# Two adjacency layers on one core: 66 tiles of the last stretch as three products of high and low halves

## What is computed

```
h  = relu(layernorm(x));   h1 = h @ W0 + B
S  = exp(-(1/adj - 1/mu)^2 / (2 sigma^2)) where adj < 0.5 off the diagonal, else 0
x1 = x + S @ h1
h  = relu(layernorm(x1));  h2 = h @ W1^T
out = x1 + (adj * adj + I) @ h2
```

## Time and profile before

| | us |
|---|---|
| median of 3 runs | 1929.82 (1929.51 to 1930.9) |
| the profiled execution | 1930.87 |
| its span | 1929.1 |
| TensorE busy (PE) | 1875.5 (97%) |
| weight loads (PEld, beside PE) | 845.5 (44%) |
| VectorE busy (DVE) | 1657.0 (86%) |
| ScalarE busy (ACT) | 1680.9 (87%) |
| DMA, over the span | 493.9 MB, 256 GB/s |

### The profile page before, as it was taken

The page is one execution under the profiler, slowest core; times in us unless marked ns, Lnnn a source line. Parts: engine busy times, 40 slices in busy tenths (PEclk is TensorE's granted clock), DMA queues, the critical chain, the costliest instruction groups (busy, mean ns, idle before and its releaser), DMA issues.

```text
span 1929.1 us, 12935 instructions
## 1 busy us (share of the span) xinstructions
PE 1875.5 (97%) x4576; PEld 845.5 (44%) x4576; DVE 1657.0 (86%) x937; ACT 1680.9 (87%) x967; POOL 87.3 (5%) x165
## 2 busy tenths in 40 slices
PE   7987989999999999999999999999999999999998
PEld 4543434444444444444444444444444444444443
DVE  7999999999999999999999999999999656556444
ACT  7999999999999999999999999999999755555421
POOL 0000000000000000000000000000000000000011
PEclk9999999999999999999999999999999999999999
DMA  7566677867877777766567766756555667877796
GB/s 265 197 223 234 246 290 258 296 249 287 291 291 272 292 267 266 260 236 251 218 250 267 258 248 216 262 194 234 195 195 197 241 262 270 317 276 297 265 371 237
DMA packets 78960, 493.90 MB, mean 256 GB/s; under 512 B 10160, under 2 KB 10544, under 8 KB 24880
## 3 DMA queue, kind: packets, MB, share of 16 engines
q1 hardware_dynamic: 66096, 451.11, 63.8%
q0 software_dynamic: 12800, 41.95, 5.7%
HBM read 469.96 MB, written 23.07 MB: 256 GB/s over the span
## 4 chain that ended last, share of the span: by engine, by line
ACT 63%; PE 27%; issue 5%; DVE 3%; DMA 1%; POOLq 0%; POOL 0%; SPq 0%; DVEq 0%
ACT rings L669 20%; ACT rings L674 19%; ACT rings L679 18%; PE p_x L415 14%; PE p_own L415 5%; PE p_l1b L397 4%; ACT rings L686 3%; PE p_l1a L397 2%; DVE rings L541 1%; DVE rings L548 1%; PE p_l1a L415 1%; DVE rings L559 1%; DMA x_buf<-xT 1%; ACT rstd_buf L715 0%; ACT rstd_buf L713 0%
## 5 line engine op out<-in xcount | busy, mean ns | idle before, releaser
L548 DVE SCALAR_TENSOR_TENSOR rings<-rings,small 128x2048 f32<-128x2048 f32 x256 | 600.0, 2344 | 56.1 <-ACT rings L674 55.1
L679 ACT ACTIVATE rings<-rings,small 128x2048 f32<-128x2048 f32 x256 | 532.6, 2080 | 63.5 <-DVE rings L548 63.5
L541 DVE SCALAR_TENSOR_TENSOR rings<-rings 128x2048 f32<-128x2048 f32 x256 | 584.4, 2283 | 0.6
L415 PE MATMUL p_x<-rings,h 128*128 128x512 f32 x1208 | 539.3, 596 | 10.2 <-DVE xa_buf L622 5.2
L669 ACT ACTIVATE rings<-rings,small 128x2048 f32<-128x2048 f32 x256 | 509.2, 1989 | 8.0 <-DVE rings L541 6.9
L559 DVE TENSOR_TENSOR rings<-rings 128x2048 f32<-128x2048 f32 x170 | 388.1, 2284 | 127.2 <-PE p_x L415 72.0
L674 ACT ACTIVATE rings<-rings 128x2048 f32<-128x2048 f32 x256 | 487.7, 1905 | 4.9
L397 PE MATMUL p_l1b<-rings,h 128*128 128x512 f32 x1024 | 464.3, 598 | 14.9 <-ACT rings L679 14.7
L397 PE MATMUL p_l1a<-rings,h 128*128 128x512 f32 x1024 | 461.0, 595 | 5.0 <-ACT rings L679 3.9
L415 PEld LDWEIGHTS p_x<-rings,h 128*128 128x128 f32 x1208 | 230.7, 191 | 302.8 <-issue 290.9
L415 PE MATMUL p_own<-rings,h 128*128 128x512 f32 x784 | 351.9, 592 | 0.0
(11 more groups left out here) (73 smaller groups left out, 327.5 us busy)
## 6 DMA issues: line engine op xcount, KB each, us to landing
rings<-adjT SPq DMA_DIRECT2D x422, 1024.0 KB, 5.3
xa_buf<-acc_dram POOLq DMA_DIRECT2D x61, 256.0 KB, 5.7
acc_dram<-xa_buf POOLq DMA_DIRECT2D x56, 256.0 KB, 5.5
x_buf<-xT SPq DMA_DIRECT2D x32, 256.0 KB, 5.1
outT<-xa_buf POOLq DMA_DIRECT2D x16, 256.0 KB, 5.3
acc_dram<-y_buf POOLq DMA_DIRECT2D x15, 256.0 KB, 6.0
y_buf<-acc_dram POOLq DMA_DIRECT2D x11, 256.0 KB, 5.5
acc_dram<-x_buf POOLq DMA_DIRECT2D x1, 256.0 KB, 5.9
```

The source lines that it names most:

```text
L415: last = pe.matmul(out[:, :], h2[:, it.source * G + g, :], block_of(q_ring, it.m % Q_RING, g), start=(it.first and g == 0), stop=(it.last ...
L541: dve.scalar_tensor_tensor(out=tile(s_ring, t % S_RING), in0=tile(a_ring, slot), scalar=CUTOFF, in1=tile(a_ring, slot), op0=ALU.is_lt, op1 ...
L548: dve.scalar_tensor_tensor(out=v, in0=v, scalar=neg_2c, in1=v, op0=ALU.add, op1=ALU.mult).then_inc(squared, 1)
L679: act.activation(v, v, ACT.Exp, bias=exp_bias, scale=neg_k).then_inc(sens_done, 1)
```

## The change

In the last stretch some items are *split*. f32r is a 4-byte type that TensorE multiplies in one pass at lower precision. For a split item, ScalarE writes Square of the tile rounded to f32r ("high", `high_half`) into a ring of three; the full f32 square goes to the q ring as before; VectorE subtracts high from it in place, rounded to f32r ("low", `low_half`). TensorE then makes three f32r products per block, h_high x high, h_high x low and h_low x high: twelve matmuls instead of four f32 ones. h2 of sources 10 to 15 is split in the same way (`split_h2`), each once.

The space: in row 15 layer 1 uses three of its seven s slots (`DENSE_RING`). Of the other four, three hold high halves and one the halves of two blocks of h2; the other h2 halves lie over blocks of h1 that layer 1 has used.

Around it: in the last row the own item of source J stands at step J; squares from step 240 on go to VectorE for m % 5 in (0, 2), not for every even m; final chains are evicted three items after their last one, not one.

The diff, cut to its core:

```diff
+LAST = S_STEPS - NC
+DENSE_RING = 3
+DENSE_SLOT = LAST % S_RING
+SPLIT_STEP = {10: 3, 11: 3, 13: 5, 12: 7, 14: 12, 15: 16}
+SPLIT_AT = {i: [J for J in SPLIT_STEP if SPLIT_STEP[J] == i] for i in SPLIT_STEP.values()}
+SPLIT_ORDER = list(SPLIT_STEP)
...
+        if c == NC - 1:
+            own_at = {J: J for J in own}
...
-        it.by = "act" if it.m % 2 else "dve"
+        it.by = "dve" if it.m % 5 in (0, 2) else "act"
...
+SPLITS = [it for it in ITEMS if it.step >= LAST + SPLIT_STEP.get(it.source, STEPS) and it.row != it.source]
...
+def slot_of(t):
+    return t % S_RING if t < LAST else DENSE_SLOT + (t - LAST) % DENSE_RING
...
-    ch.evac = max(ch.last_m + (1 if ch.final else EVAC), CHAINS[ch.index - 1].evac if ch.index else 0)
+    ch.evac = max(ch.last_m + EVAC, CHAINS[ch.index - 1].evac if ch.index else 0)
...
                         sp.wait_ge(q_by[it.by], it.squares)
+                        if it.split is not None:
+                            sp.wait_ge(high_ready, it.split + 1)
...
+            def l2_split(it):
+                out = p_own[it.row % 2] if it.own else p_chain[it.chain.bank]
+                pe.wait_ge(h_split, SPLIT_ORDER.index(it.source) + 1)
+                pe.wait_ge(low_ready, it.split + 1)
+                for g in range(G):
+                    high = high_ring[it.split % 3][:, g * CHUNK:(g + 1) * CHUNK]
+                    low = low_ring[it.m % Q_RING][:, g * CHUNK:(g + 1) * CHUNK]
+                    h_high, h_low = h2_high[it.source][:, g, :], h2_low[it.source][:, g, :]
+                    pe.matmul(out[:, :], h_high, high, start=(it.first and g == 0), stop=False)
+                    pe.matmul(out[:, :], h_high, low, start=False, stop=False)
+                    last = pe.matmul(out[:, :], h_low, high, start=False, stop=(it.last and g == G - 1))
+                last.then_inc(q_used, 1)
...
-                if t >= S_RING:
+                if t >= LAST + DENSE_RING:
+                    dve.wait_ge(s_used, t - DENSE_RING + 1)
+                elif t >= S_RING:
                     dve.wait_ge(s_used, t - S_RING + 1)
...
+            def low_half(it):
+                if it.by == "dve":
+                    dve.wait_ge(q_by["dve"], it.squares)
+                else:
+                    dve.wait_ge(q_by["act"], it.squares)
+                dve.wait_ge(high_ready, it.split + 1)
+                dve.tensor_tensor(low_ring[it.m % Q_RING][:, :], tile(q_ring, it.m % Q_RING),
+                                  high_ring[it.split % 3][:, :].bitcast(F32),
+                                  ALU.subtract).then_inc(low_ready, 1)
+
+            def split_h2(J):
+                n = SPLIT_ORDER.index(J)
+                dve.wait_ge(s_used, LAST if n < 2 else LAST + 2 * (n - 1))
+                dve.wait_ge(h2_ready, J + 1)
+                rows = slice(J * G, (J + 1) * G)
+                dve.tensor_copy(h2_high[J][:, :, :], h2[:, rows, :]).then_inc(h_high_done, 1)
+                dve.wait_ge(h_high_done, n + 1)
+                dve.tensor_tensor(h2_low[J][:, :, :], h2[:, rows, :], h2_high[J][:, :, :].bitcast(F32),
+                                  ALU.subtract).then_inc(h_split, 1)
...
+                for J in SPLIT_AT.get(s - LAST, []):
+                    if s < S_STEPS:
+                        split_h2(J)
                 for it in AT_STEP[s]:
                     if it.by == "dve":
                         square_adj(it)
+                    if it.m and ITEMS[it.m - 1].split is not None:
+                        low_half(ITEMS[it.m - 1])
+                    if it.step == S_STEPS + TAIL + OPEN + 1:
+                        split_h2(NC - 1)
                     for ch in EVAC_AFTER.get(it.m, []):
                         add_chain(ch)
...
+            def high_half(it):
+                slot = it.load % A_RING
+                act.wait_ge(a_loaded[slot], a_rounds(it.load))
+                if it.split < 3:
+                    act.wait_ge(s_used, LAST)
+                else:
+                    act.wait_ge(q_used, SPLITS[it.split - 3].m + 1)
+                act.activation(high_ring[it.split % 3][:, :], tile(a_ring, slot),
+                               ACT.Square).then_inc(high_ready, 1)
...
                     if it.by == "act":
                         square_adj(it)
+                    if it.split is not None:
+                        high_half(it)
```

More of the change, by code:

```diff
@@ L8 @@
 F32 = mybir.dt.float32
+F32R = mybir.dt.float32r
 P = 128
@@ L152 @@
     it.squares = Q_COUNT[it.by]
+SPLITS = [it for it in ITEMS if it.step >= LAST + SPLIT_STEP.get(it.source, STEPS) and it.row != it.source]
+for it in ITEMS:
+    it.split = None
+for r, it in enumerate(SPLITS):
+    it.split = r
+def slot_of(t):
+    return t % S_RING if t < LAST else DENSE_SLOT + (t - LAST) % DENSE_RING
 for it in ITEMS:
@@ L194 @@
 for ch in CHAINS:
-    ch.evac = max(ch.last_m + (1 if ch.final else EVAC), CHAINS[ch.index - 1].evac if ch.index else 0)
+    ch.evac = max(ch.last_m + EVAC, CHAINS[ch.index - 1].evac if ch.index else 0)
     ch.store = ch.evac + 0.5
-    EVAC_AFTER.setdefault(min(ch.evac, len(ITEMS) - 1), []).append(ch)
+    EVAC_AFTER.setdefault(min(ch.evac, len(ITEMS)), []).append(ch)
     TRANSFERS.append((ch.store, 0, ch.index))
@@ L237, in gnn_program, with over, slot_at @@
         a_ring, q_ring, s_ring = 0, A_RING, A_RING + Q_RING
+        rings_at = nc.sbuf_base - 4 * (A_RING + Q_RING + S_RING) * TILE
+        h1_at = rings_at - 8 * NC * G * D
+        def over(name, shape, place):
+            return nc.alloc_sbuf_tensor_at(name, shape, F32R, offset=place)
+        def slot_at(ring, slot):
+            return rings_at + 4 * (ring + slot) * TILE
+        low_ring = [over(f"low{n}", [P, TILE], slot_at(q_ring, n)) for n in range(Q_RING)]
+        high_ring = [over(f"high{n}", [P, TILE], slot_at(s_ring, (DENSE_SLOT + DENSE_RING + n) % S_RING))
+                     for n in range(3)]
+        h_parts_at = slot_at(s_ring, (DENSE_SLOT + DENSE_RING + 3) % S_RING)
+        h2_high, h2_low = {}, {}
+        for n, J in enumerate(SPLIT_ORDER):
+            place = h_parts_at + 8 * n * G * D if n < 2 else h1_at + 8 * (n - 2) * G * D
+            h2_high[J] = over(f"h2_high{J}", [P, G, D], place)
+            h2_low[J] = over(f"h2_low{J}", [P, G, D], place + 4 * G * D)
         x_buf = [sb(f"x_buf{n}", [D, CHUNK]) for n in range(2)]
@@ L280, in gnn_program @@
         q_used = sem("q_used")
+        high_ready = sem("high_ready")
+        low_ready = sem("low_ready")
+        h_high_done = sem("h_high_done")
+        h_split = sem("h_split")
         node_centred = sem("node_centred")
@@ L396, in l1 @@
                 for g in range(G):
-                    last = pe.matmul(p_l1[c % 2][:, :], h1[:, J * G + g, :], block_of(s_ring, t % S_RING, g),
+                    last = pe.matmul(p_l1[c % 2][:, :], h1[:, J * G + g, :], block_of(s_ring, slot_of(t), g),
                                      start=(i == 0 and g == 0), stop=(i == NC - 1 and g == G - 1))
                 last.then_inc(s_used, 1)
+            def l2_split(it):
[10 more added lines that the diff above has]
+                last.then_inc(q_used, 1)
             def l2(it):
@@ L410, in l2 @@
                     pe.wait_ge(xa_added, it.chain.after[-1].index + 1)
+                if it.split is not None:
+                    l2_split(it)
+                    return
                 pe.wait_ge(h2_ready, it.source + 1)
@@ L538, in premask @@
                     dve.wait_ge(diag_marked, marks[0])
-                if t >= S_RING:
+                if t >= LAST + DENSE_RING:
+                    dve.wait_ge(s_used, t - DENSE_RING + 1)
+                elif t >= S_RING:
                     dve.wait_ge(s_used, t - S_RING + 1)
-                dve.scalar_tensor_tensor(out=tile(s_ring, t % S_RING), in0=tile(a_ring, slot), scalar=CUTOFF,
+                dve.scalar_tensor_tensor(out=tile(s_ring, slot_of(t)), in0=tile(a_ring, slot), scalar=CUTOFF,
                                          in1=tile(a_ring, slot), op0=ALU.is_lt,
@@ L546, in square @@
                 dve.wait_ge(recip_done, t + 1)
-                v = tile(s_ring, t % S_RING)
+                v = tile(s_ring, slot_of(t))
                 dve.scalar_tensor_tensor(out=v, in0=v, scalar=neg_2c, in1=v, op0=ALU.add,
@@ L649, in _ @@
                         square_adj(it)
+                    if it.m and ITEMS[it.m - 1].split is not None:
+                        low_half(ITEMS[it.m - 1])
+                    if it.step == S_STEPS + TAIL + OPEN + 1:
+                        split_h2(NC - 1)
                     for ch in EVAC_AFTER.get(it.m, []):
                         add_chain(ch)
+                    if it.m == len(ITEMS) - 1:
+                        if it.split is not None:
+                            low_half(it)
+                        for ch in EVAC_AFTER.get(it.m + 1, []):
+                            add_chain(ch)
                 if 3 <= s < NC + 3:
```

## The result

| | us | ratio to before |
|---|---|---|
| before, median of 4 | 1929.78 | |
| after, median of 4 (1985.5 to 1989.31) | 1988.8 | 1.0301, 95% interval 1.0286 to 1.0316 |
| the profiled execution of after, its span | 1989.31, 1987.5 | |

The kernel became 59 us slower. The forecast was 27.6 us slower, with 1985 as the upper end: the sign and the mechanism were right, the size forecast was less than half of the one measured.

A forecast was written before the change was run, and what follows sets the result against it. TensorE, busy 97% of the span, was taken as the bound. Balances of -2.9, +10, +10.9, +5 and +2.4 (+25.4 us) plus +2.2 for the clock gave +27.6: 1957.5 us against the median, range 1922 to 1985.

The forecast's parts named there:

- the clock: TensorE's granted clock falls to half after long waits; of six such waits one drop counted in full, +2.2 us.
- the walk: Queue-by-queue reckoning of TensorE's waits less split savings, from row 15's step 3 to the tail's end: +25.4 us.
- What binds: TensorE, busy 97%, bounds the kernel; its savings count only as far as VectorE and ScalarE can follow.
- Where the waits fall: TensorE's waits listed by item: 18.5 us in steps 8 to 10, 26.0 in steps 11 to 15.
- A product: One single-pass matmul of a split tile on TensorE takes 0.215 us with its weight load overlapped; twelve take 2.59.
- the rival of loads that don't hide: TensorE's weight loads don't overlap products: 4.86 us a split tile, +94 us, 2024; chance 0.07, shared with products not single-pass.
- At nothing: Parts priced at no cost: three layer-1 slots, the own tiles' order, later evictions; adj loads covered, thinly in the tail.
- VectorE running ahead: Rival: late low halves cost nothing, only engine sums count; -19 us at best, 1911 to 1922; chance 0.18.
- tiles of adj: Rival: with DMA near its limit they arrive late, every tail item 0.3 us later, +8 us, 1966; chance 0.04.
- The clock rival: TensorE's clock drops at all six long waits, nothing absorbs it: 11 us above the forecast, 1968; chance 0.06.

The follow-up runs named there:

- the clock kept: Changed kernel with 66 f32 matmuls that nothing reads (the dummies) put in TensorE's queue ahead of the low halves it waits for: 1973.86 us, ratio 1.0224.

## Why the prediction was right in kind and half in size

The mechanism came as forecast, and two terms of the sum were sized wrong: the clock (+2.2 said, at least 15 measured) and the walk (+25.4 said, at most 43 measured).

- *What binds.* Right: TensorE's saving counts only as far as VectorE follows. The run without subtractions shows the turn from -22 to +59.
- *Where the waits fall.* Right, item by item. Of the 18 waits up to step 15 listed in the prediction, 16 are in the trace (not those of 190 and 199), and most within 0.6 us: 191 waits 1.84 (1.4 said), 192 2.15 (2.5), 196 2.00 (2.1), 197 3.70 (4.1), 204 2.03 (2.2), 214 2.50 (2.4), 221 2.74 (2.8). 201, 205, 209, 213 and 217 are 0.7 to 1.9 shorter, 176 is 4.13 for 2.2. Two small ones more, at 182 and 183. In the tail each five items have two of 2.0 us.
- *The clock.* This step failed: "I count one drop in full, +2.2". Of the changed kernel's 792 f32r products at least 116 ran at half clock, 0.43 us apart instead of 0.23, which alone is 23 us; keeping the clock gives back 15. In the tail I had counted no drop, and there five of the eleven waits of 1.65 to 2.13 us had the clock at 0.50 within 1.5 us of their end. The line shows it behind the one that ended at 1918.04; the five items over it take 19.75 us instead of 18.25.

```profile
1920.00:1922.00 2.00, 2.00 (x6) 1.56 (x5) 2.00 (x3) 0.00 (x0) 1.01 (x2) 0.50 1.00 397
```

- *The walk's sum.* This term failed as well: +25.4 was said, and with the clock kept the kernel is 43 us slower than before (1973.86 against 1930.41), part of which can be delay by the dummies. The middle came out: from layer-1 tile 8 to tile 14 the walk has 118.2 us (17.17 x 6 + 15.2 of its balances), the run with the clock kept 120.2. The rest is off in two places. Up to tile 8 the run stands 6 us behind the walk. Of that, 2.4 are in the step of item 176: low half 175, ahead of it in the queue, was 1.8 us late for its high half on ScalarE. Another 1.8 are in the step of 182 and 183, for which the walk had no wait. And from tile 14 to TensorE's end it takes 143.5 us against 133.8. Of these 9.7, 3.7 lie ahead of item 230 (the changed kernel itself, without dummies, is 1.9 over the walk there) and 6.1 behind it. There each bound cycle holds products, and these were priced too low (next point). The walk also spread VectorE's squares evenly, two in five, but those of the diagonals 253 and 255 are VectorE's too and make 252 and 254 wait, 2.13 and 2.04 us in the changed kernel.
- *A product.* 0.215 us was taken, 0.228 is measured (2.73 us a tile), with 190 ns of weight load beside it. It is the overlap that the rows showed, and the rival of loads that don't hide fell. The Trainium skill's rule ("TensorE: Matmul & The Clock Gate", section "The mechanism"), that a weight load overlaps matmuls only in other row groups, doesn't hold in this trace; the other case that the section names, a load into the background weight buffer, would allow what is seen. In the tail two items take 7.72 us instead of 7.4, five 18.25 instead of 17.6: 26 items +3.4. I do not know what the 13 ns are.
- *At nothing.* Right for the three slots, the order and the evictions (ratio 1.0002). Wrong for DMA: 98% busy at 376 GB/s was no limit yet, 417 is reached with fewer splits.
- *The rivals.* VectorE running ahead was refuted: the waits behind low halves return in almost every step. That the ring of three lets no lead build up is the likely reason; no run changed the ring. The prediction's sum for it has a slip: with half the lead of 11 us lost it comes to -14, and -8 is the whole lead lost. No wait for tiles of adj is seen in the changed kernel from 1640 us on; they show in the faster ones (without subtractions, and with 35 splits). The clock rival, priced at +11, came nearest, with drops in more places than its six, and still leaves the 18 us by which the walk's sum was short.

## What to carry to other kernels

Before work is moved from a full engine to half empty ones, walk the queues: an instruction that waits for the full engine, put ahead of the one that the full engine waits for, costs its length in each cycle whatever the shares say. Then price each wait so found twice, once as idle time and once as the time at half clock that may follow it; here waits of 2 us were enough for it in five of eleven cases. And let the consumer do first what doesn't need the late operand: with the same work this alone was worth 31.5 us. Together with a choice of items that keeps VectorE's squares from standing ahead of most low halves, half of the splits gave a gain.

## What the runs showed of the hardware

- An f32r product of 512 columns takes 0.228 us at full clock, 0.43 at half, each with its own weight load hidden (190 ns at full clock, 330 at half); an f32 one takes two records of 0.429 us.
- Rounding 128x512 f32 to f32r from SBUF takes VectorE 0.42 us, a subtraction of the same size 0.69.
- The granted clock fell to 0.50 behind a wait of 2.03 us that ended at 1918.04, 7.7 us after another; it held through a like pair at 1892.07 and 1899.79 (2.03 and 1.94 us), and through the one wait of 2.03 us at 1739.12. What tells these apart was not tried.
- In the run with 35 splits DMA moved 417 GB/s over 40 us in the tail at a busy share of 1.01, where 376 had shown as 0.98.
